# GAT chunk weights made by ScalarE instead of VectorE, and ScalarE's row copies moved ahead of the exponentials

## The reference

```python
xw = x @ W
xj = xw[src].reshape(-1, H, D) + edge_emb.reshape(-1, H, D)
alpha = leaky_relu(einsum(xw[dst], att_i) + einsum(xj, att_j), 0.2)
amax = segment_max(alpha, dst)
ea = exp(alpha - amax[dst])
denom = segment_sum(ea, dst)
msg = xj * (ea / (denom[dst] + EPS))[..., None]
h = segment_sum(msg, dst).mean(axis=1) + b
```

## Time and profile before

| what | value |
|---|---|
| time, median of 3 runs | 3885.16 us (3884.87 to 3886.05) |
| span of the profiled execution | 3885.4 us |
| PE busy | 2467.2 us, 63% |
| DVE busy | 2253.0 us, 58% |
| POOL busy | 2210.1 us, 57% |
| ACT busy | 711.4 us, 18% |
| chain that ended last, by engine | DVE 41%, PE 24%, issue 20%, unknown queue 8% |

### The profile page before, as it was taken

How to read it: one execution, slowest core, us unless ns; L and a number is a source line. 1 busy time by engine, 2 the same in 40 slices (tenths; PEclk the granted TensorE clock), 3 DMA queues, 4 the chain that set the end, 5 groups by cost and what they waited for, 6 DMA issues and landing times.

```text
span 3885.4 us, 47078 instructions
## 1 busy us (share of the span) xinstructions
PE 2467.2 (63%) x13212; PEld 2001.4 (52%) x13212; DVE 2253.0 (58%) x7877; ACT 711.4 (18%) x3102; POOL 2210.1 (57%) x2355
## 2 busy tenths in 40 slices
PE   7778726566592666659275755926676592757558
PEld 6668615454461555547164544615454461545446
DVE  9966636555572655657265555725555572655556
ACT  0067521111121111112111111211111121111111
POOL 0066466666616666661666666266666626766661
PEclk8555555555565555556555555655555565555556
DMA  3212022222202222220222222022222202222221
GB/s 105 87 58 78 22 58 53 51 53 57 49 18 49 53 52 50 57 50 18 49 53 51 53 57 49 18 50 53 51 53 57 48 18 50 53 53 51 52 45 34
DMA packets 114128, 195.69 MB, mean 50 GB/s; under 512 B 39897, under 2 KB 77272, under 8 KB 113864
## 3 DMA queue, kind: packets, MB, share of 16 engines
q0 software_dynamic: 62560, 130.25, 14.7%
q1 hardware_dynamic: 51304, 62.42, 5.1%
HBM read 180.86 MB, written 11.67 MB: 50 GB/s over the span
## 4 chain that ended last, share of the span: by engine, by line
DVE 41%; PE 24%; issue 20%; another core or an unknown queue 8%; DVEq 5%; ACTq 1%; ACT 1%; POOL 0%; DMA 0%; POOLq 0%
PE bank L719 11%; DVE acc L1177 8%; PE bank L721 5%; DVEq L992 3%; PE bank L698 2%; PE bank L727 2%; DVE ai_win L1065 2%; DVE alpha L1068 2%; DVE pw L1135 2%; PE bank L745 2%; DVE into L1117 2%; DVEq L1177 1%; DVE prod L1046 1%; DVE fwd L1124 1%
## 5 line engine op out<-in xcount | busy, mean ns | idle before, releaser
L498 POOL DMA_INDIRECT ring<-table,srci x1955 | 1941.1, 993 | 958.3 <-issue 558.7
L719 PE MATMUL bank<-pw,ring 128*128 128x48 f32 x3910 | 1263.3, 419 | 998.7 <-issue 496.1
L719 PEld LDWEIGHTS bank<-pw,ring 128*128 128x128 f32 x3910 | 1014.6, 314 | 1182.6 <-issue 835.1
L1177 DVE TENSOR_TENSOR acc<-acc,bank 128x72 f32 x1955 | 448.5, 229 | 806.8 <-remote 269.6
L721 PE MATMUL bank<-onehot,est 128*36 128x24 f32 x3910 | 626.0, 244 | 162.2 <-issue 161.9
L721 PEld LDWEIGHTS bank<-onehot,est 128*36 128x36 f32 x3910 | 387.7, 149 | 333.8 <-issue 163.4
L568 ACT COPY ai_win<-ai_rows 128x48 f32 x1955 | 350.4, 229 | 572.4 <-issue 550.1
L574 ACT ACTIVATE dd<-dd 128x66 f32<-128x66 f32 x75 | 19.4, 258 | 2072.1 <-DVE dd L1128 1183.1
L505 POOL TENSOR_TENSOR S<-S 128x128 f32<-128x128 f32 x125 | 57.4, 459 | 403.1 <-ACT S L578 398.7
L480 POOL TENSOR_TENSOR ring<-ring,acc 128x512 f32<-128x512 f32 x98 | 114.7, 1172 | 269.9 <-ACT ring L533 266.6
L762 PE MATMUL bank<-Wl,S 128*128 128x258 f32 x250 | 153.8, 708 | 70.7 <-issue 45.6
(11 more groups left out here) (206 smaller groups left out, 2570.9 us busy)
## 6 DMA issues: line engine op xcount, KB each, us to landing
ring<-table,srci POOLq DMA_INDIRECT x1955
ai_rows<-lo_dram SPq DMA_DIRECT2D x28, 896.0 KB, 4.3
at<-in_attr SPq DMA_DIRECT2D x65, 224.0 KB
table<-ring SPq DMA_DIRECT2D x15, 390.0 KB, 3.7
table<-ring SPq DMA_DIRECT2D x5, 325.0 KB, 3.2
result<-ring SPq DMA_DIRECT2D x24, 64.0 KB
x_mid<-ring SPq DMA_DIRECT2D x3, 384.0 KB, 2.7
table<-ring SPq DMA_DIRECT2D x5, 130.0 KB, 2.3
```

Source lines behind the costliest of these rows:

```text
L498: nc.gpsimd.indirect_dma_start(out=ring[:, slot(t), :], out_offset=None, in_=table, in_offset=bass.IndirectOffsetOnAxis(ap=srci[:, t:t + 1 ...
L719: nc.tensor.matmul(o[:, 0:H * WIN], ring[:, slot(t), 0:D], pw[:, g % DEEP, k, :, :].rearrange("p h w -> p (h w)"), start=True, stop=True)
L1177: V.tensor_tensor(win, win, grp_sum(g, k).rearrange("p (r w) -> p r w", r=REG), ALU.add)\
```

## The change

Weights are made by ACT, one operation per tile and head (128x24, the one-hot times that edge's probability as a per-partition scale), 56 in a full chunk. DVE's `weigh` and its call sites go. `chain_probs` raises a new semaphore `probs_sb` as soon as the probabilities stand in `est`. ACT copies the windows of chunk c+1 before the exponential of chunk c, no longer behind it. Buffers and banks are counted over all layers (`gg`), and PE gets waits of its own for `est` and for the addition that frees its bank.

```diff
@@ scalar
+            def weights(layer, c):
+                act.wait_ge(probs_sb, layer * NC + c + 1)
+                for g in GC[c]:
+                    _, t, n = GROUPS[g]
+                    gg = layer * G + g
+                    if gg >= DEEP:
+                        act.wait_ge(sums, gg - DEEP + 1)
+                    for k in range(n):
+                        for h in range(H):
+                            p = est[:, c % 2, t - TC[c] + k, HF + h:HF + h + 1]
+                            ins = nc.scalar.activation(pw[:, gg % DEEP, k, h, :], onehot[:, t + k, :], ACT.Copy, scale=p)
+                    ins.then_inc(p_ready, 1)
...
                 for c in range(NC):
-                    exps(layer, c)
                     if c + 1 < NC:
                         windows(layer, c + 1)
+                    exps(layer, c)
+                    weights(layer, c)
@@ tensor, aggregate
                 pe.wait_ge(p_ready, gg + 1)
+                if g == GC[c][0]:
+                    pe.wait_ge(est_ready, layer * NC + c + 1)
+                if gg >= DEEP:
+                    _, t_old, n_old = GROUPS[(gg - DEEP) % G]
+                    pe.wait_ge(added, (gg - DEEP) // G * REAL + t_old + n_old)
@@ vector
-            def weigh(layer, g):
...
-                done = mark(V.tensor_copy(es[:, :, HF:HF + H], pr))
+                V.tensor_copy(es[:, :, HF:HF + H], pr).then_inc(probs_sb, 1)
...
-                v.wait_ge(step, done)
-                for g in GC[c][0:2 if c else AHEAD]:
-                    weigh(layer, g)
...
-                        if i + AHEAD < n_groups:
-                            weigh(layer, GC[c][i + AHEAD])
...
-                        if more and i == n_groups - 1:
-                            for ahead in GC[c + 1][2:AHEAD]:
-                                weigh(layer, ahead)
```

More of the change, by code:

```diff
@@ L79, in act_groups @@
     return sum(not pool_group(k) for k in range(g + 1))
-AHEAD = 4
 SUM_BANKS = (0, 1, 2, 4, 5, 6)
@@ L259, in gcn_sum, with grp_sum @@
             return bank[g % 3][:, k * WIN:(k + 1) * WIN]
-        def grp_sum(g, k):
-            return bank[SUM_BANKS[g % DEEP]][:, k * REG * WIN:(k + 1) * REG * WIN]
+        def grp_sum(gg, k):
+            return bank[SUM_BANKS[gg % DEEP]][:, k * REG * WIN:(k + 1) * REG * WIN]
         loaded = sem("loaded")
@@ L331, in program @@
         exp_al = sem("exp_al")
+        probs_sb = sem("probs_sb")
         p_ready = sem("p_ready")
@@ L717, in aggregate @@
                 for k in range(n):
-                    o, t = grp_sum(g, k), t0 + k
+                    o, t = grp_sum(gg, k), t0 + k
                     nc.tensor.matmul(o[:, 0:H * WIN], ring[:, slot(t), 0:D],
-                                     pw[:, g % DEEP, k, :, :].rearrange("p h w -> p (h w)"), start=True, stop=True)
+                                     pw[:, gg % DEEP, k, :, :].rearrange("p h w -> p (h w)"), start=True, stop=True)
                     ins = nc.tensor.matmul(o[0:EC, H * WIN:REG * WIN], est[:, c % 2, t - TC[c], :], onehot[:, t, :],
@@ L1130, in chain_cols @@
                 link(V.transpose(maxes[:, :, :], fwd[:, :, :]))
-            def weigh(layer, g):
-                c, t, n = GROUPS[g]
-                k = t - TC[c]
-                V.tensor_tensor(pw[:, g % DEEP, 0:n, :, :],
-                                onehot[:, t:t + n, :].unsqueeze(2).broadcast_to((P, n, H, WIN)),
-                                est[:, c % 2, k:k + n, HF:HF + H].unsqueeze(3).broadcast_to((P, n, H, WIN)), ALU.mult)\
-                    .then_inc(p_ready, 1)
             def chain_probs(layer, c):
@@ L1176, in add_group @@
                         v.wait_ge(added, layer * REAL + t + k)
-                    V.tensor_tensor(win, win, grp_sum(g, k).rearrange("p (r w) -> p r w", r=REG), ALU.add)\
+                    V.tensor_tensor(win, win, grp_sum(layer * G + g, k).rearrange("p (r w) -> p r w", r=REG), ALU.add)\
                         .then_inc(added, 1)
@@ L1208, in _ @@
                     scan_at, rows_at, probs_at = chain_at(c)
-                    n_groups = len(GC[c])
                     for i, g in enumerate(GC[c]):
```

## The result

The changed kernel takes **3924.32 us** (median of 4 runs, 3916.53 to 3932.25) where the kernel before took 3885.01 beside it (4 runs, 3880.55 to 3886.05): a ratio of 1.0109, 95% interval 1.0091 to 1.0127. It is slower by about 39 us where 3 us less were forecast. Run again beside other variants it came to 1.0131 (1.0088 to 1.0174).

A forecast was written before the change was run, and what follows sets the result against it. The prediction took POOL's own gather pace plus two pauses a chunk to bound the kernel. From 3885.4 us, +5.5 for the hand-off at layer edges and -9 for POOL's port gave 3882 us, range 3845 to 3985.

The forecast's parts named there:

- The period: Inside a layer, POOL's 35.0 us of gathers plus two pauses make a chunk of 40 to 41 us; chance 0.50.
- The first rival: DVE's chain sets the period: each chunk gains 0.81 us and loses 0.43, giving 3868 us; chance 0.23.
- 56 operations on ACT: Weights on ACT at 0.20 us each: 1.6 us per group of eight, 11.2 a chunk, ahead of PE after the first group.
- The slower rival: ACT makes weights in slow steps of 0.7 us, costing 1.5 us a chunk: 3981 us; chance 0.27.
- The hand-off: Probabilities to PE's first product: 0.43 us later a chunk, free inside the gathers, +5.5 us at the layers' edges.
- The order of the copies: ACT's 28 copies ahead of the exponential should be through when it is wanted: worth 0, up to 1 us delay covered.
- PE's new waits: PE's waits for `est` and for the addition are for things done earlier: worth 0.
- POOL and the port: Without DVE's weights, POOL's gathers are held less: 0.15 us a chunk over 60 chunks, -9 us.

The follow-up runs named there:

- e15: Kernel before with DVE's seven weight products per chunk cut to 2 values a partition, order of copies unchanged: 3902.61 us, ratio 1.0013.
- e8: Changed kernel with the weights of each chunk's first two groups made by DVE again, the rest by ACT: 3941.28 us, ratio 1.0094.
- e1: Kernel before with only ACT's copies for the next chunk moved ahead of this chunk's exponential, weights still on DVE: 3902.39 us, ratio 1.0020.
- e16: Kernel before with ACT's copies moved ahead of the exponential and DVE's weight products cut to 2 values a partition: 3925.44 us, ratio 1.0070.
- e10: Kernel before with copies ahead of the exponential, 56 ACT scalings nobody waits for behind it, and four `pw` buffers, not six: 3930.57 us, ratio 1.0063.
- e17: Changed kernel with ACT's order exponential, weights of three groups, copies for the next chunk, other weights: 3905.02 us, ratio 1.0045.
- e13: Kernel before with only the change's two new PE waits added: 3880.60 us, ratio 1.0000.
- e4: Changed kernel with one more DVE operation per chunk, about 0.3 us, behind group 0's additions: 3935.10 us, ratio 1.0085.
- e6: Changed kernel with DVE's three long products per chunk cut into two or three pieces: 3924.15 us, ratio 1.0069.
- e7: Kernel before with DVE's three long products per chunk cut into two or three pieces: 3891.66 us, ratio 0.9990.
- e5: Changed kernel with a DVE operation of about 0.3 us at each of the seven places of the old weight products: 3937.81 us, ratio 1.0084.
- e11: Kernel before with a POOL wait for an earlier addition ahead of the 13th gather in chunks 3 to 12: 4096.76 us, ratio 1.0554.
- e14: Kernel before with a POOL wait for an earlier addition ahead of the 9th gather in chunks 3 to 12: 4365.61 us, ratio 1.1252.

## Why the prediction was wrong

- **The period** ("POOL's own pace plus two pauses is the period, and a group done 1 us sooner or later changes nothing"): right in what it was used for. DVE's relief is worth nothing (e15), and the hand-off costs nothing inside the gathers (e8). It was wrong to treat the pauses as given. Their number (124, then 112 and 137 in two traces of the changed kernel) and their length changed with nearly every variant, which the last sentence of the prediction named as what would make it wrong altogether.
- **The first rival** (DVE's chain sets the period, faster): no. Relieving DVE gives nothing (e15). In these two kernels a slow chain mostly ends with POOL's pause, whenever DVE comes to it: of the chains over 7 us in chunks 2 to 11, 36 of 46 before and 32 of 34 after the change end within 3 us of a pause's end. In e15 only 5 of 42 do, so that is not the whole reason.
- **56 operations on ACT**: sized right. Eight take 1.6 to 1.7 us (24 in 5.03, 56 in 11.82). **The slower rival**, slow steps among the weights, hit the sign by another way than it names. Some weights do fall into slow steps (123 of 3910 follow the one before by more than 0.35 us, where 0.21 is usual). But a chunk's first four groups follow each other on PE by 3.36, 4.11 and 3.56 us before and by 3.36, 4.15 and 3.35 us after (means of chunks 2 to 11), and PE idles only 3.4 us between them in 50 chunks, so they don't wait for weights. That the time lies inside the stated range is luck: the range reached so far up for this rival's sake.
- **The hand-off**: 1.64 to 2.08 us from the start of the copy to the first product, 0.44 where 0.43 was forecast; the edges cost 5.6 to 5.7 us where 5.5 stood, all of it between the first products of chunks 12 and 14:

```profile
3188.55 0.18 DVE L1157 COPY est<-probs 128x22 f32<-128x22 f32 x1
```

```profile
3190.57 0.66 PE L738 MATMUL bank<-pw,ring 128*128 128x48 f32 x2 [2.41 <-ACT pw L586]
```

  1.84 us from the copy's end, 0.84 before. At chunk 0 the hand-off is 2.2 us from the start of the copy, where it was 1.7 to 5.0, so it costs nothing there; what chunk 0 loses, it loses to the order of the copies.
- **The order of the copies** ("they should be through. Worth 0"): **this is the step that failed.** The copies were asked only whether they are through when the exponential is wanted, and only for a chunk inside a layer. There they mostly are (the exponential waits 4.9 us in all 50 chunks 2 to 11, 18.8 before), though they begin 15 us after the first product, inside the slow stretch, and not where they were. In chunk 0 of each layer they aren't: its exponential waits 85.5 and 48.7 us in the two traces (8.0 before), and POOL 64.5 and 73.0 us ahead of the 61st gathers (60.9). By itself the order costs 0.2% (e1); together with the relief (e16, 0.7%), with more ACT work (e10, 0.63%) or with both it costs more, and moving the copies gives back over half of the loss by the medians (e17).
- **PE's new waits**: 0, as said (e13).
- **POOL and the port** (-9 us): wrong in sign, held time rose by 31 and 23 us in two traces. The weights never held POOL much (8 of the 101 gathers that begin during one are over 1.05 us). They kept a long product away from the beginning of a gather (e4). On the time it is some tenths of a percent at most (e6, e7).

**What stays open.** Why order, relief and ACT's work cost so much more together than alone. How much of the loss is the layers' starts and how much the chunks inside was not separated by a run. ACT's 56 operations without the changed order, with nobody waiting for them, were not run. The long chains are not the whole way: e5 and e6 have 5 and 0 of them, fewer than the kernel before, and still lose 0.7 to 0.8%; e1 has 32 and loses 0.2%. What makes the slow steps isn't named by any row; the DMA packets that the trace marks as instruction lie beside only 14 of the 378 slow steps of the chains before.

## What to carry to other kernels

Where engines run in slow stretches that some other engine's pause ends, work moved within a chunk can cost by where it lands, not by its busy time: put beside each other, before the change, what each engine does in the slow stretch. Before moving an operation off an engine, make it almost free in place and time that; here it would have said in one run that there was nothing to win. And an order that is changed along the way needs a run of its own, with and without the rest: here moving the copies gave back more than half of the loss by the medians. An order that is harmless inside a loop needs a look at the loop's first turn, where what stood between two steps is missing.

## What the runs showed of the hardware

- **Which DVE operations hold a gather.** In the trace of before, of the gathers that begin during the product of rows and one-hots 65 of 65 are over 1.05 us, during the score product 49 of 57, during the product for `est` 46 of 57, but none of 21 during the reduction of the scores (1.01 us long), none of 112 during the reduction of the windows (1.54 us) and 1 of 221 during the additions, which read PSUM. The Trainium skill says so (SBUF — State Buffer, "Who interferes with whom"): a VectorE instruction with two SBUF inputs contends with GpSimd's reads, a reduction never does. The trace agrees, and adds that what it costs depends on where in the product the gather begins: 1.17 or 2.21 us for the same product.
- **Slow steps are longer beside ACT's.** A slow step of DVE's chain (next instruction 0.6 to 3 us after it; ACT's: 0.55 to 1.6 us) takes 1.17 us on average in the kernel before, where none of 378 lies beside slow steps of ACT, and 1.44 us for the 303 of the changed kernel that do (1.25 for its 96 others). In e1 it is 272 at 1.42 against 58 at 1.23.
- **A pause of POOL clears it**: with a pause put ahead of the chain (e11, e14) DVE's chain takes 5.2 to 5.5 us in all 50 chunks of both traces, where it took 5.3 to 14.7 us before and up to 20.9 us in the changed kernel.
